# Regrouping a mixture-of-experts stage behind graph attention: two chunks and one, in place of one and two

## The chip, the cores and the metric

The kernel runs on one core of a Trainium2 chip, as one program and one launch. The metric is the device time in microseconds (us) of one execution; lower is better. Three timed runs of the kernel before gave 534.91, 538.07 and 540.5 us, so the median is 538.07 us. One more execution was recorded by the hardware profiler; every duration below comes from that one.

The engines are called as in the profile: PE (TensorE; PEld is its weight load), DVE (VectorE), ACT (ScalarE), POOL (GpSimd) and SP (SyncE, which here only issues DMAs).

## The reference, cut to what matters

A stack of four residual layers works on 1354 nodes with 128 features; `adj` is a 1354 x 1354 matrix of edge weights, none negative.

```python
x = x + gnn0(layernorm(x), adj)        # weights from adj, times a message
x = x + ffn0(layernorm(x))             # 8 experts of 256, top 2, computed densely
x = x + gnn1(layernorm(x), adj)        # two GRU cells and three heads of attention
x = x + ffn1(layernorm(x))             # 8 experts of 341, top 2

def ffn1(z):
    probs = softmax(z @ router_w.T)
    p, idx = top_k(probs, 2)
    p = p / (sum(p) + 1e-9)
    gates = one_hot(idx) weighted by p
    h = silu(z @ w1[e].T) * (z @ w3[e].T)
    return sum over e of gates[e] * (h @ w2[e].T)
```

The change concerns the last layer, `ffn1`, and how it is laid beside the attention of `gnn1`.

## The kernel before, in words

Nodes are columns. They are cut into 11 tiles of 128 (the last has 74), and the tiles into three chunks: chunk 0 is tiles 0 to 3, chunk 1 tiles 4 to 7, chunk 2 tiles 8 to 10 (330 columns). The names `mid(1, c)`, `center(3, c)` and the like carry the layer and the chunk.

**Attention.** The loop has 3 chunks x 3 heads x 11 tiles = 99 steps. A step (h, j) is one `factor` matmul on PE (L1310), one `numerator` on DVE (L2029, which multiplies by the adjacency) and one `attend` on PE (L1321, recorded as two MATMULs). `factor` runs three steps ahead; DVE writes into a ring of three. Steps (0, j) to (5, j) are chunks 0 and 1 with 512 columns, steps (6, j) to (8, j) are chunk 2 with 330. Everything else is hung onto these steps by tables written out by hand: `MAIN_PE` and `MAIN_DVE` say after which step a side task runs on its engine, and `MAIN_ACT` is ACT's plain order. Engines run in order, so a side task that waits holds up the steps behind it. Side tasks are the GRU of the node update (`gates`, `mid`, `new`, `blend`, `add`), then for each chunk the layer norm (`mean`, `center`, `var`, `scale`), the router (`logits`, `scores`, `shares`, `ranks`, `picks`, `weights`), the token-major copy (`ztok`), the counting of places (`prefix`, `slots`) and a list of blocks (`list`). `support` copies the finished sum of a chunk out of PSUM, and the first step of the next chunk waits for it.

**Experts.** Each token goes to two experts. POOL writes its row with an indirect DMA into a table in DRAM, sorted by expert: `send(t, j)` for tile t and choice j (L568). When all sends of a group of tokens have landed and its `list` is known, SP loads the table block by block, 128 rows each, at most four blocks ahead (`block_load`, L466). A block is transposed (L1377 on PE, L2047 on DVE), multiplied by w1 and w3 (L1385, L1386), goes through `silu` on ACT (L895) and a product on DVE (L2065), is transposed (L1392, L885) and multiplied by w2 (L1401). DVE scales the result by the gate (L2052, L2053) and POOL scatters it into a second table (`block_sent`, L574). In iteration b, PE does the first products of block b, then the transposes of block b + 2, then the later steps of blocks b - 1 and b - 2. The first five blocks share one pair of PSUM banks, so there the first products wait for DVE's product of the block before.

There are two groups, each with its own tables and list. Before, group 0 is chunk 0 (15 blocks) and group 1 chunks 1 and 2 (21 blocks). Chunk 1's last steps, all of chunk 2's last GRU part and both routers run beside the blocks by six further tables (`PE1A`, `PE1B` and so on, keyed by block). `SENDS` says after which block's scatter POOL makes which sends: two after each of blocks 0 to 3 and 5 to 7. At the end a group's results are read back (`fetched`, `picked_y`) and `combine` adds them to the residual (L2039, L2042); SP writes the output.

What orders the work around the change is therefore only this: the hand-written tables, each engine's own order, and semaphores. The lines of the profile that matter are L1321 and L2029 (attention), L1595 to L1664 (router, places and list), L568 and L574 (POOL), L466 (SP), L1377 to L1401 (blocks).

## Time and profile before

| what | value |
|---|---|
| median of the timed runs | 538.07 us |
| profiled execution, its own time | 539.31 us |
| span of its record | 537.6 us |
| PE busy | 449.4 us (84%) |
| DVE busy | 345.5 us (64%) |
| ACT busy | 239.4 us (45%) |
| POOL busy | 68.8 us (13%) |

The profiled execution is 1.7 us longer than its span, which is what lies around the recorded instructions, and 0.23% above the median. Busy shares are averages over all stages. The attention's last chunk runs from about 367 to 410 us, the blocks of the experts from 413 to 523 us, and the rest is the way out. PEclk in a table is the clock granted to PE, 1.00 for 2.4 GHz and 0.50 for 1.2 GHz. An idle time in square brackets stands before the instruction, with what ended it.

### The profile page before, as it was taken

Reading aid. Unit: us, or ns where it says so; the run is one execution under the profiler, and the core shown is the slowest. Engines: PE = TensorE matmul, PEld = TensorE weight load, DVE = VectorE, ACT = ScalarE, POOL = GpSimd, SP = SyncE. Lnnn points to the kernel's source line nnn. Section 1 sums busy time; section 2 is a strip of 40 time slices with the busy share of each in tenths; the row PEclk is TensorE's granted clock in tenths of the full one; section 3 lists DMA queues with packets and bytes.
Section 4 is the critical chain, followed back from the end, with each engine's and each line's share of the span. In section 5 each row is a group of like instructions: output and inputs, shape, how many; then the busy total and the mean of one; then the engine's idle time right before and its main releaser. Section 6 shows DMA issues by size and latency. Waiting matters only on the chain.

```text
span 537.6 us, 6518 instructions
## 1 busy us (share of the span) xinstructions
PE 449.4 (84%) x1858; PEld 265.5 (49%) x1858; DVE 345.5 (64%) x761; ACT 239.4 (45%) x389; POOL 68.8 (13%) x115
## 2 busy tenths in 40 slices
PE   4497679978699899989889999998799858799980
PEld 2432435535356654546434444344456546588860
DVE  0997989868478742446737877866777636355541
ACT  4988789587685522040350212212122462344430
POOL 5000000000010000000000000000140255444440
PEclk9779698989899999999999999999989979899995
DMA  8989200000000000000000004400010111123213
GB/s 283 312 262 390 84 0 0 1 0 1 1 1 1 2 0 1 0 2 1 1 0 1 0 30 160 125 20 8 11 46 15 36 54 46 43 61 99 79 37 109
DMA packets 26491, 31.22 MB, mean 58 GB/s; under 512 B 3572, under 2 KB 20781, under 8 KB 26453
## 3 DMA queue, kind: packets, MB, share of 16 engines
q1 hardware_dynamic: 23557, 26.52, 15.6%
q0 software_dynamic: 1984, 3.78, 2.1%
q10 hardware_dynamic: 912, 0.46, 0.3%
q8 instruction: 19, 0.31, 0.2%
q14 instruction: 19, 0.16, 0.1%
HBM read 19.44 MB, written 11.31 MB: 57 GB/s over the span
## 4 chain that ended last, share of the span: by engine, by line
PE 52%; DVE 24%; ACT 10%; issue 9%; another core or an unknown queue 2%; DMA 1%; POOL 1%; DVEq 0%; POOLq 0%; ACTq 0%; SPq 0%
PE bank L1321 10%; PE bank L1130 4%; PE bank L1401 4%; PE bank L1385 4%; PE bank L1269 3%; PE bank L1386 3%; DVE pr_ring L2029 3%; PE bank L1310 2%; DVE y_units L1510 2%; PE bank L1091 2%; DVE y_units L1521 2%; PE bank L980 2%; PE bank L1392 2%; DVE hr_ring L1832 2%
## 5 line engine op out<-in xcount | busy, mean ns | idle before, releaser
L1321 PE MATMUL bank<-pr_ring,hW 128*128 128x512 f32 (+3 forms) x198 | 95.0, 565 | 8.1 <-DVE pr_ring L2029 6.4
L2029 DVE SCALAR_TENSOR_TENSOR pr_ring<-adjT,regR,bank 128x512 f32<-128x512 f32 (+3 forms) x99 | 65.0, 680 | 33.2 <-PE bank L1310 31.4
L1321 PEld LDWEIGHTS bank<-pr_ring,hW 128*128 128x128 f32 (+1 forms) x198 | 35.2, 195 | 36.7 <-issue 17.5
L980 PE MATMUL bank<-y_units,msg 128*128 128x512 f32 (+3 forms) x66 | 33.2, 632 | 15.7 <-DVE y_units L1531 15.7
L1091 PE MATMUL bank<-hr_ring,W2s 128*128 128x512 f32 (+1 forms) x96 | 44.9, 555 | 0.0
L574 POOL DMA_INDIRECT yg<-pr_ring,goes x36 | 34.8, 966 | 72.9 <-DVE pr_ring L2053 71.7
L1832 DVE TENSOR_TENSOR hr_ring<-hr_ring,bank 128x512 f32<-128x512 f32 (+1 forms) x48 | 29.5, 620 | 19.3 <-ACT hr_ring L774 15.6
L2065 DVE TENSOR_TENSOR hbuf<-hbuf,bank 128x341 f32<-128x341 f32 x36 | 18.3, 509 | 33.3 <-issue 15.5
L774 ACT ACTIVATE hr_ring<-bank,b1c 128x512 f32<-128x512 f32 (+1 forms) x48 | 29.8, 628 | 14.2 <-PE bank L953 14.1
L951 PE MATMUL bank<-zhi,W1hi 128*128 128x512 f32 (+1 forms) x48 | 34.7, 723 | 1.2 <-ACT hr_ring L774 0.9
L1401 PE MATMUL bank<-wall,hturned 114*128 (+1 forms) x216 | 31.0, 280 | 1.0 <-DVE pr_ring L2053 0.9
L568 POOL DMA_INDIRECT xg<-rowx,slot x22 | 22.5, 1024 | 65.1 <-DVE slot L1642 59.0
L1385 PE MATMUL bank<-wall,xturned 128*128 x72 | 28.4, 477 | 1.4 <-DVE xturned L2047 0.6
L885 ACT COPY hturned<-bank 114x384 f32<-114x384 f32 x36 | 17.2, 479 | 26.2 <-PE bank L1392 18.2
L1401 PEld LDWEIGHTS bank<-wall,hturned 114*128 114x128 f32 (+1 forms) x216 | 27.6, 195 | 1.7 <-issue 1.7
L980 PEld LDWEIGHTS bank<-y_units,msg 128*128 128x128 f32 (+1 forms) x66 | 13.5, 218 | 28.3 <-DVE y_units L1531 19.7
L1386 PE MATMUL bank<-wall,xturned 128*128 x72 | 27.1, 458 | 0.0
L895 ACT ACTIVATE hbuf<-bank 128x341 f32<-128x341 f32 x36 | 16.4, 457 | 24.0 <-PE bank L1385 21.8
L1130 PE MATMUL bank<-adjT,hTok 128*128 128x512 f32 (+3 forms) x66 | 26.2, 545 | 0.0
L538 POOL TENSOR_SCALAR_AFFINE_SELECT adjT<-adjT 128x128 f32<-128x128 f32 (+1 forms) x11 | 3.4, 323 | 156.4 <-DVE y_units L1531 135.7
L635 ACT ACTIVATE y_units<-y_units,one 128x1024 f32<-128x1024 f32 (+3 forms) x18 | 17.6, 979 | 11.6 <-DVE y_units L1521 11.6
L1510 DVE SCALAR_TENSOR_TENSOR y_units<-adjT,y_units 128x1024 int32<-128x1024 int32 (+3 forms) x18 | 18.2, 1014 | 5.2 <-ACT y_units L630 5.2
(308 smaller groups left out, 879.3 us busy)
## 6 DMA issues: line engine op xcount, KB each, us to landing
xg<-zeros SPq DMA_DIRECT2D x1, 4095.0 KB
wall<-in_w SPq DMA_DIRECT2D x2, 1364.0 KB
adjT<-in_adjT SPq DMA_DIRECT2D x1, 2560.0 KB
xg<-zeros SPq DMA_DIRECT2D x1, 2535.0 KB
xblk<-xg SPq DMA_DIRECT2D x36, 65.0 KB
adjT<-in_adjT SPq DMA_DIRECT2D x1, 1650.0 KB
adjT<-in_adjT SPq DMA_DIRECT2D x3, 512.0 KB, 5.8
adjT<-in_adjT SPq DMA_DIRECT2D x1, 1024.0 KB
```

The costliest lines, as they stand in the source:

```text
L574: pool.indirect_dma_start(yg_d[g], bass.IndirectOffsetOnAxis(goes[:, b % YRING:b % YRING + 1], 0), yblk[:, b % YRING, :], None).then_inc(s ...
L774: nc.scalar.activation(hr_ring[:, q % RING0, 0:w], B_H[q % 3][:, 0:w], ACT.Relu, bias=b1c[:, e * M0 + m:e * M0 + m + 1]).then_inc(s["h_rel ...
L951: nc.tensor.matmul(out, whi, xhi, start=start, stop=False)
L980: mm = nc.tensor.matmul(B_GNN[:, 0:w], msg[0:r, j, :], y_units[0:r, g % RINGY, i, 0:w], start=(j == 0), stop=(j == T - 1))
L1091: nc.tensor.matmul(B_Y0[:, 0:w], W2s[:, e, m, :], hr_ring[:, q % RING0, 0:w], start=False, stop=(e == E - 1 and m == M0 - 1)).then_inc(s[" ...
L1130: ns = nc.tensor.matmul(B_NS[c][:, 0:width(c)], hTok[0:r, j, :], adjT[0:r, j, cols(c)], start=(j == 0), stop=(j == T - 1))
L1321: nc.tensor.matmul(B_ACC[:, 0:w], hW[0:r, j, k * P:(k + 1) * P], ring[0:r, 0:w], start=(k == 0 and j == 0), stop=(k == K - 1 and j == T - ...
L1385: nc.tensor.matmul(B_H1[pair(b)][:, 0:H1], x, walls[:, bass.ds(base, H1)], start=True, stop=True).then_inc(s["h1_ps"], 1)
L1386: nc.tensor.matmul(B_H3[pair(b)][:, 0:H1], x, walls[:, bass.ds(base + H1, H1)], start=True, stop=True).then_inc(s["h3_ps"], 1)
L1401: mm = nc.tensor.matmul(B_Y[:, 0:P], hturned[0:r, b % 2, k * P:(k + 1) * P], walls[0:r, bass.ds(base + 2 * H1 + k * P, P)], start=(k == 0) ...
L1832: nc.vector.tensor_tensor(hr, hr, B_GATE[q // M0 % 2][:, 0:w], ALU.mult).then_inc(s["h_gated"], 1)
L2029: nc.vector.scalar_tensor_tensor(out=pr_ring[0:r, 4 + p % R_RING, 0:w], in0=adjT[0:r, j, cols(c)], scalar=g_col[0:r, j, k:k + 1], in1=B_F[ ...
```

## The change

1. The groups become tiles 0 to 7 (chunks 0 and 1, 23 blocks) and tiles 8 to 10 (chunk 2, 13 blocks). There are still 36 blocks. The first group's results are fetched and combined at block 31 and 30 in place of 25 and 24, for eight tiles in place of four; the last `combine` takes three tiles, once, in place of four and three.
2. The router of this layer is shorter. `shares` is gone (the two largest shares are found from the logits and only their exponentials are divided by their sum), `ranks` has three instructions in place of five, the copy of the logits out of PSUM is gone, and `weights` has one more.
3. Chunk 1's last side tasks, `ztok`, `prefix`, `ranks`, `picks`, `weights`, `slots`, and the list of group 0 move from the blocks into the attention, as do chunk 1's eight sends. Chunk 0's move to earlier steps. The list is cut in two tasks, `starts` and `list`.
4. The last chunk's GRU (`last_gates`, `mid(1, 2)`) goes ahead of the first block on PE, DVE and ACT.
5. POOL makes the last chunk's six sends one at a time, after the scatters of blocks 8, 10, 12, 14, 16 and 18.

```diff
-GROUPS = [(0, 4), (4, T)]
-GROUP_OF = [0, 1, 1]
+GROUPS = [(0, 8), (8, T)]
+GROUP_OF = [0, 0, 1]
-FETCH = BLOCKS[0] + 10
+FETCH = BLOCKS[0] + 8
 MAIN_PE = {
-    (5, 10): [("ztok", 0)], (6, 4): [("gates", 1, 1)], (6, 6): [("mid", 1, 1)], (6, 8): [("prefix", 0)],
-    (7, 4): [("mean", 3, 1)], (7, 8): [("var", 3, 1)], (8, 5): [("logits", 4)],}
+    (5, 1): [("ztok", 0)], (5, 3): [("prefix", 0)], (6, 0): [("gates", 1, 1)], (6, 2): [("mid", 1, 1)], (6, 8): [("mean", 3, 1)],
+    (7, 0): [("var", 3, 1)], (7, 4): [("logits", 4)], (7, 5): [("ztok", 1)], (7, 7): [("prefix", 1)]}
 MAIN_DVE = {
...
-    (6, 9): [("mid", 1, 1)], (7, 0): [("weights", 3), ("slots", 3), ("list", 0)], (7, 2): [("blend", 1, 1)], (7, 4): [("add", 1, 1)], (7, 6): [("center", 3, 1)],
+    (6, 5): [("mid", 1, 1)], (6, 8): [("blend", 1, 1)], (6, 9): [("add", 1, 1)], (7, 1): [("center", 3, 1)], (7, 5): [("scale", 3, 1)],
+    (7, 8): [("scores", 4), ("ranks", 4), ("picks", 4)], (7, 10): [("weights", 4)], (8, 1): [("slots", 4)], (8, 3): [("starts", 0)], (8, 6): [("list", 0)]}
...
-PE1A = {0: [("mid", 1, 2)], 1: [("prefix", 1)], 4: [("var", 3, 2)], 7: [("prefix", 2)]}
-PE1B = {0: [("ztok", 1)], 3: [("mean", 3, 2)], 5: [("logits", 5), ("ztok", 2)], 9: [("xtok", 0)], 10: [("xtok", 1)], 11: [("xtok", 2)]}
+PE1A = {4: [("var", 3, 2)], 7: [("prefix", 2)]}
+PE1B = {3: [("mean", 3, 2)], 5: [("logits", 5), ("ztok", 2)], 9: [("xtok", 0)], 10: [("xtok", 1)], 11: [("xtok", 2)]}
-DVE1A = {0: [("mid_n", 1, 2)], 1: [("blend", 1, 2), ("add", 1, 2)], 3: [("slots", 4)], 6: [("ranks", 5), ("picks", 5)], 7: [("slots", 5)]}
+DVE1A = {0: [("blend", 1, 2)], 1: [("add", 1, 2)], 5: [("scores", 5), ("ranks", 5), ("picks", 5)], 7: [("slots", 5)]}
-SENDS = {b: [(4 + b, 0), (4 + b, 1)] for b in range(4)}
-SENDS.update({5 + i: [(8 + i, 0), (8 + i, 1)] for i in range(3)})
+SENDS = {8 + 2 * i: [(8 + i // 2, i % 2)] for i in range(6)}
...
-            for t in tiles(0):
+            for t in range(8):
                 for j in range(2):
                     send(t, j)
...
                 pe.wait_ge(s["tables_in"], 64 + 80)
+                last_gates()
+                mid(1, C - 1)
                 pe.wait_ge(s["list_set"], 1)
...
             def route_ranks(n):
...
+                if l:
+                    link(nc.vector.tensor_tensor(g4[0], D.unsqueeze(2).to_broadcast([P, k, E, E]), D.unsqueeze(3).to_broadcast([P, k, E, E]), ALU.subtract))
+                    link(nc.vector.tensor_tensor(g4[1], g4[0], floor1[:, :, :].unsqueeze(1).to_broadcast([P, k, E, E]), ALU.is_gt))
+                    link(nc.vector.tensor_reduce(G, g4[1], AX.X, ALU.add))
+                    return
```

On POOL, first the order before, from the end of the constants. `xg<-rowx,slot` is a send, `yg<-pr_ring,goes` the scatter of a block.

```order
L578 MEMSET place_no 128x4x8 x2
L568 DMA xg<-rowx,slot 4992x130 x8
L574 DMA yg<-pr_ring,goes 2304x128
L568 DMA xg<-rowx,slot 8064x130 x2
L574 DMA yg<-pr_ring,goes 2304x128
L568 DMA xg<-rowx,slot 8064x130 x2
L574 DMA yg<-pr_ring,goes 2304x128
L568 DMA xg<-rowx,slot 8064x130 x2
L574 DMA yg<-pr_ring,goes 2304x128
L568 DMA xg<-rowx,slot 8064x130 x2
L574 DMA yg<-pr_ring,goes 2304x128 x2
```

And the order on POOL after the change, from the same place.

```order
L574 TENSOR_SCALAR floor<-tri 128x64
L563 DMA xg<-rowx,slot 9088x130 x16
L569 DMA yg<-pr_ring,goes 2560x128 x9
L563 DMA xg<-rowx,slot 3968x130
L569 DMA yg<-pr_ring,goes 2560x128 x2
L563 DMA xg<-rowx,slot 3968x130
L569 DMA yg<-pr_ring,goes 2560x128 x2
L563 DMA xg<-rowx,slot 3968x130
L569 DMA yg<-pr_ring,goes 2560x128 x2
L563 DMA xg<-rowx,slot 3968x130
L569 DMA yg<-pr_ring,goes 2560x128 x2
L563 DMA xg<-rowx,slot 3968x130
```

Sixteen sends now stand ahead of the first scatter, and of the last group's six each has two scatters before the next; the sixth (not shown) follows the scatter of block 18.

On DVE, before the change, chunk 1's `blend` (L1922 to L1924) and `add` (L1930, L1931) in the attention, with the numerators L2029 around them.

```order
L2029 SCALAR_TENSOR_TENSOR pr_ring<-adjT,regR,bank 128x330 x2
L1922 TENSOR_TENSOR nsT<-zT,ge 128x512
L1923 SCALAR_TENSOR_TENSOR nsT<-ge,nsT 128x512
L1924 SCALAR_TENSOR_TENSOR nsT<-nsT,ge 128x512
L2029 SCALAR_TENSOR_TENSOR pr_ring<-adjT,regR,bank 128x330 x2
L1930 TENSOR_TENSOR nsT<-nsT,bank 128x512
L1931 TENSOR_TENSOR xT<-xT,nsT 128x512
```

The same piece of DVE's order after the change.

```order
L2029 SCALAR_TENSOR_TENSOR pr_ring<-adjT,regR,bank 128x330 x3
L1922 TENSOR_TENSOR nsT<-zT,ge 128x512
L1923 SCALAR_TENSOR_TENSOR nsT<-ge,nsT 128x512
L1924 SCALAR_TENSOR_TENSOR nsT<-nsT,ge 128x512
L2029 SCALAR_TENSOR_TENSOR pr_ring<-adjT,regR,bank 128x330
L1930 TENSOR_TENSOR nsT<-nsT,bank 128x512
L1931 TENSOR_TENSOR xT<-xT,nsT 128x512
```

One numerator now stands between `blend` and `add` in place of two; PE's `mean(3, 1)`, which waits for `add`, is placed after step (6, 8), one step ahead of `add`'s step, where before both stood at (7, 4).

## Rows read from the trace of the kernel before

**Rows 1.** Windows by stage: us, busy (count) of PE PEld DVE ACT POOL; PEclk, DMA, GB/s.
```profile
367.20:409.55 42.35, 36.63 (x149) 20.85 (x147) 31.60 (x82) 10.15 (x13) 8.16 (x8) 0.92 0.07 20
413.20:467.90 54.70, 41.01 (x243) 29.69 (x242) 27.88 (x105) 23.24 (x42) 23.97 (x24) 0.91 0.15 43
467.90:523.10 55.20, 54.29 (x337) 43.38 (x336) 27.56 (x96) 22.05 (x48) 24.12 (x25) 1.00 0.24 67
```

**Rows 2.** Timeline (start, us, engine, what): the list inside the attention, PE's stop.
```profile
382.82 0.22 DVE L1595 TENSOR_TENSOR chosen<-rt,place_no 128x64 f32<-128x64 f32 x1
...
388.37 0.92 PE L1321 MATMUL bank<-pr_ring,hW 128*128 128x330 f32 x1 [3.53 <-DVE pr_ring L2029]
```

**Rows 3.** Windows: the stretch behind that stop.
```profile
388.40:394.40 6.00, 6.00 (x13) 3.07 (x14) 5.62 (x10) 0.00 (x0) 4.58 (x5) 0.50 0.14 45
```

**Rows 4.** Timeline: start of chunk 2's steps, blend, add, two ordinary steps.
```profile
369.42 0.82 PE L1321 MATMUL bank<-pr_ring,hW 128*128 128x330 f32 x2 [1.59 <-ACT nsT L880]
...
388.72 0.67 DVE L1922 TENSOR_TENSOR nsT<-zT,ge 128x512 f32<-128x512 f32 x1
...
392.53 0.69 DVE L1931 TENSOR_TENSOR xT<-xT,nsT 128x512 f32<-128x512 f32 x1
...
400.98 0.30 PE L1310 MATMUL bank<-share_c,pr_ring 120*128 120x330 bf16 x1
...
401.68 0.30 PE L1310 MATMUL bank<-share_c,pr_ring 120*128 120x330 bf16 x1
```

**Rows 5.** Timeline of PE: first products of blocks 0, 4, 6, 13, 35.
```profile
413.18 0.45 PE L1385 MATMUL bank<-wall,xturned 128*128 x1
...
426.84 0.55 PE L1385 MATMUL bank<-wall,xturned 128*128 x1
...
439.72 0.93 PE L1385 MATMUL bank<-wall,xturned 128*128 x1
...
467.94 0.45 PE L1385 MATMUL bank<-wall,xturned 128*128 x1
...
517.53 0.46 PE L1385 MATMUL bank<-wall,xturned 128*128 x1
```

**Rows 6.** Chain of waits (start, us, what) in the first 14 blocks.
```profile
435.15 3.03 another core or an unknown queue
...
453.50 2.88 another core or an unknown queue
...
456.79 1.71 another core or an unknown queue
458.55 3.55 another core or an unknown queue
```

**Rows 7.** Windows: the stretch of blocks 4 to 12; the eight sends inside the attention.
```profile
426.80:462.10 35.30, 24.64 (x147) 17.46 (x147) 16.38 (x66) 14.59 (x24) 21.07 (x21) 0.90 0.17 49
386.40:396.80 10.40, 8.43 (x21) 4.33 (x22) 8.80 (x21) 0.63 (x1) 8.16 (x8) 0.67 0.14 45
```

**Rows 8.** Timeline: first and last of eight sends in a row, first block load.
```profile
386.44 1.23 POOL L568 DMA_INDIRECT xg<-rowx,slot  x1 [56.87 <-DVE slot L1642]
...
395.77 0.96 POOL L568 DMA_INDIRECT xg<-rowx,slot  x1 [0.30 <-issue]
...
399.12 0.38 SPq L466 DMA_DIRECT2D xblk<-xg  x1
```

**Rows 9.** Timeline: the scatter of block 11, two iterations later.
```profile
471.10 0.96 POOL L574 DMA_INDIRECT yg<-pr_ring,goes  x1 [1.30 <-DVE pr_ring L2053]
```

**Rows 10.** Timeline: the last scatter, the fetch, the start of combine, the last store.
```profile
523.86 0.96 POOL L574 DMA_INDIRECT yg<-pr_ring,goes  x1 [0.67 <-DVE pr_ring L2053]
...
526.39 0.38 SPq L480 DMA_DIRECT2D picked_y<-yg  x1
...
531.59 0.69 DVE L2039 TENSOR_TENSOR answer<-x3tok,picked_y 128x512 f32<-128x512 f32 x1 [8.01 <-DMA picked_y<-yg]
...
534.52 0.39 SPq L486 DMA_DIRECT2D out<-answer  x1
```

91 lines of the change are left out of this document (41 added, 50 removed).

## The prediction, made before the changed kernel was run

> **What bounds the kernel now.** I read the stage windows first, then the timeline of PE at each stage's borders, then the chain of waits inside the stage that looks worst. The windows [rows 1] show three stages. In the attention of the last chunk PE is busy 36.63 of 42.35 us, so PE sets the pace and every wait of PE costs about its length. In the first thirteen blocks PE is busy 41.01 of 54.70 us, so something else sets the pace. From block 13 on it is busy 54.29 of 55.20: pure PE, and the side tasks that remain there are hidden. The same shows in the block starts [rows 5]: 22 blocks from 467.94 to 517.53 are 2.25 us each, while the first 13 took 54.8 us, 25.5 more than 13 such blocks. The chain of waits says where much of that is [rows 6]: four times PE's work stands still for "another core or an unknown queue", 3.03 + 2.88 + 1.71 + 3.55 = 11.2 us. Nobody else works on this program. All four stand where POOL makes sends and scatters without a pause: 21 indirect DMAs in 35.3 us, 21.07 us busy [rows 7], and with the 0.30 us of issue in front of each [rows 8] that is 27.4 us, 78%. I read them as one thing: while POOL issues such a run, signals that PE sent earlier arrive late. That is an inference; the rows show only the place and the length.
>
> Inside the attention there is one plain stop [rows 2]: DVE starts weights, slots and the list of group 0 at 382.82 in one piece, and PE runs dry for 3.53 us until the numerator behind them. The six us after it run at clock 0.50 with PE busy throughout [rows 3], so half of that, 3.0 us, is lost too.
>
> **The change, part by part**, against the profiled execution's 539.31 us.
>
> *(a) The attention, chunk 2.* Out go the stop (-3.5), the slow clock behind it (-3.0), and most of the 1.59 us wait at the first step of the chunk [rows 4], since chunk 0's tasks on ACT come earlier (-1.2). In come `ztok` and an eight-tile `prefix` on PE, about ten small matmuls that overlap; from 0.30 us for one [rows 4] less the overlap I take 1.35 us, plus 0.4 for fewer steps between the waits. New waits: `mean(3, 1)` now stands on PE after step (6, 8), and `blend` starts on DVE only after that step's numerator. Between them lie three operations of blend, one numerator and two of add. A 512-wide operation is 0.67 to 0.69 us [rows 4], so about 5 x 0.67 + 0.5 = 3.9 us, while PE has three steps in hand at 0.70 us each (401.68 less 400.98 [rows 4]), the first partly spent: about 2.65 us of waiting. The DVE work moved in (route of chunk 1, slots, list) is split into pieces of about 1 to 3 us against PE's 2.1 us of steps in hand: 0.6 for `var`, 1.1 before `logits`, 1.1 for `ztok`, 1.0 for weights and slots, and 1.9 for `list`, whose one piece is the longest left. Together 8.4; each could be 0 if DVE is further ahead than I count, or 1.5 times as large, so 4 to 11. Sum of (a): -7.7 + 1.75 + 8.4 = **+2.5**. The attention ends at 412.1 and not at 409.55.
>
> *(b) End of the attention to the first product.* Before 3.63 us (413.18 [rows 5] less 409.55 [rows 1]). The slots of chunk 1 are ready at about 403.1. Eight sends took 386.44 to 395.77 for the start of the last, 9.33 us, and SP's first load came 3.35 us after that [rows 8]. So the last send starts at about 412.9, counting about half a microsecond in which POOL waits for DVE, the load is issued at 416.3, and with about 2.7 us for landing and the transpose the first product is at 419. `last_gates` and `mid(1, 2)`, about 5.6 us on PE with their waits, fill that gap up to 417.7; they cost nothing more, and would cost their length if the sends were early. Between 2 (sends in time) and 7 (POOL late), I take **+3.3**.
>
> *(c) Blocks 0 to 13.* Chunk 1's eight sends leave this stage, and so do `mid`, `ztok`, `prefix` and `slots`. POOL has in blocks 0 to 8 one scatter per block, as it has after block 13, where no such wait exists. So -11.2 for the four waits and about -1.4 for ztok and prefix on PE; another -1.9 for `mid` and the waits on it. Walking through block by block gives 40.2 us in place of 54.75: 10.9 more than steady blocks, which is what the shared pair of banks (blocks 0 to 4), three means, logits and transposes of chunk 2 need. **-14.5**. If the waits belong not to the runs of sends but to this stage, 0 to -3; if the slow clock there (PEclk 0.90 [rows 7]) goes altogether, -17.
>
> *(d) The change of group.* This is what the change newly adds. The last send follows the scatter of block 18. A scatter of block b - 2 starts 3.16 us behind the first product of block b (471.10 less 467.94 [rows 9, 5]), so with T20 the first product of block 20 the send is at T20 + 4.43, the load of block 23 at T20 + 7.8 by the 3.35 us above, and its rows are transposed and ready at about T20 + 9.75. But block 23 is the first of group 1, and PE's transposes of it are queued in iteration 21, at T20 + 2.25 + 1.15 = T20 + 3.4. PE stops for 6.4 us, with the later steps of blocks 20 and 19 queued behind; blocks 24 to 26 load meanwhile, and the fetch of group 0 isn't touched. SP's latency of 3.35 was seen behind a run of sends; behind a single one it is at least 2.3, and the landing between 0 and 3.1 us (the store at the very end takes 537.6 less 534.52 [rows 10]), of which I take 2.0: the stop is between 3.4 and 8. PE ran at 0.50 for six us after the last stop of 3.5 us [rows 3], in steps that kept it busy; a similar dip here costs 0 to 3.4, I take 2.0. **+8.4**. Before, the last group's sends ended after block 7 and its first block was 15, so no such wait shows.
>
> *(e) The end.* From the last scatter 2.53 us to the fetch, 5.2 more to the first `combine`, 2.9 to the last store and 3.1 to the end [rows 10]. Three tiles in place of seven shorten the fetch by 1.55 (the fixed part stays) and leave 1.3 us less of combine: **-3.0**, between -1.5 and -4. The earlier eight-tile fetch (double the bytes at DMA share 0.24 [rows 1]) and its combine of 1024 columns, about 2.2 us on DVE, lie beside blocks in which DVE is busy only 27.56 of 55.20 us [rows 1]: nothing, and about 2 us if one of them held PE's operands back.
>
> The shorter router saves DVE work only; beside PE-bound steps it is inside (a).
>
> Sum: 2.5 + 3.3 - 14.5 + 8.4 - 3.0 = **-3.3**, so 536.0 us. The profiled execution is 0.23% above the median of the three runs, so 534.8; I say **535.0**.
>
> **A rule weighed.** In the attention eight sends ran beside DVE busy 8.80 of 10.40 us [rows 7], each 0.96 to 1.23 us, one every 1.3 [rows 8]. By that sixteen sends inside the attention are cheap. The Trainium skill, "SBUF — State Buffer", section "SBUF: two separate sides", says the opposite can happen: descriptors of a GpSimd-issued DMA can't be written while a two-port VectorE operation holds the shared ports, and a DMA of some 620 ns then took some 3100. By that rule eight sends would take about 20 us longer and the first block with them. The trace disagrees so far, so the sum goes by the row.
>
> **The rivals.**
>
> 1. *The late signals come back between blocks 8 and 18 (slower).* There POOL makes 11 scatters and 6 sends, 17 x 1.27 = 21.6 us, in 11 blocks of 2.25 = 24.8 us: 87%, denser than the 78% at which the four waits stand [rows 7]. Against it: a run is only scatter, send, scatter. The deciding point is whether the late signals follow the share of POOL or the number of DMAs without a pause. If the share, the waits return with 8 to 11.2 us: 543 to 546. Chance 0.17, with the lags that two runs of eight sends could bring into the attention's end.
> 2. *The waits in the attention are smaller, and no slow clock follows (faster).* DVE is busy 31.60 of 42.35 us [rows 1]; if its pieces fit between the steps, (a) is -2 instead of +2.5, and (d) without the dip is +6.4: 535 - 4.5 - 2 = 528.5. Chance 0.27.
> 3. *The first blocks don't get faster.* If the four waits hang on the shared banks or on list and table, (c) gives only -3.3 and the whole is 546. Chance 0.05.
> 4. *The rule above*: some 20 us late before block 0, about 550. Chance 0.02.
> 5. *The change does nothing new at the change of group*, because SP's loads don't wait for all sends: (d) is 0, 526.6. The lists need all tokens, so 0.03.
>
> **How the numbers follow.** My forecast has the rest, 0.46, with its own range 531 to 540. What a measurement of this kernel can tell from no change is about 1%, 5.4 us: below 532.7 is faster, above 543.5 slower. Faster: 0.25 of rival 2, rival 5 wholly, and 0.09 of the forecast, 0.37. Slower: 0.09 of rival 1, and 3 and 4 wholly, 0.16. The rest, 0.47, is the same. The range from 528 to 543 leaves out most of rivals 3 to 5 and the far ends of 1 and 2.
>
> **What would show it.** (a) no DVE piece from weights to list, PE idle before `mean` at about 2.6 us and before the step behind `list` below 2; (b) first product at about 419; (c) no "unknown queue" in the chain before block 8, 13 blocks in about 40 us; (d) PE idle about 6 us before the transposes of block 23, ended by DMA or DVE's copy of it, and nothing like it elsewhere; (e) last scatter to end in about 10.7 us. Wrong would be: waits of PE between blocks 8 and 18 that no send explains, a clock of 0.50 over more than ten us, or a block 23 that finds its rows there.

## The result, and the profile after

The changed kernel took 549.31 us (median of 4, 545.81 to 550.29) where the kernel before took 537.20 us (4 runs, 534.91 to 540.50): ratio 1.0216, 95% interval 1.0173 to 1.0259. I had forecast 535.0 us, range 528 to 543: the change is slower, by 1.7 to 2.6%, and the time lies outside the range. On two other chips the ratio was 1.0211 [1.0146, 1.0277] and 1.0147 [1.0097, 1.0197], slower there too.

The windows of the changed kernel by stage: us, then busy time (count) of PE, PEld, DVE, ACT and POOL, PEclk, DMA share, GB/s. They answer to [rows 1]: the attention's last chunk, blocks 0 to 13, 13 to 21, 21 to 23, and 23 to 35.

```profile
373.60:418.25 44.65, 37.92 (x167) 21.41 (x167) 29.58 (x74) 9.64 (x12) 11.22 (x13) 0.92 0.06 18
426.10:468.20 42.10, 38.02 (x200) 27.68 (x201) 22.99 (x85) 21.02 (x38) 10.53 (x11) 0.88 0.15 39
468.20:486.30 18.10, 18.10 (x115) 14.56 (x114) 9.05 (x32) 7.50 (x17) 11.67 (x12) 1.00 0.23 65
486.30:502.10 15.80, 7.64 (x30) 5.86 (x29) 2.35 (x8) 1.87 (x4) 3.54 (x4) 0.68 0.15 38
502.10:530.70 28.60, 27.58 (x170) 21.73 (x169) 15.46 (x49) 11.23 (x24) 12.22 (x12) 1.00 0.36 100
```

The first blocks are the gain: 42.1 us where [rows 1] had 54.7. The third row is as steady as before, eight blocks in 18.1 us at clock 1.00, with the single sends beside them. The fourth row is the loss: two blocks take 15.8 us, and PE is busy for half of it at clock 0.68. The chain of waits there (start, us, what) names its links, and the timeline of PE gives the stop:

```profile
487.17 0.95 POOL yg L569
488.43 4.12 DMA xg<-rowx,slot
...
493.66 2.04 DMA xblk<-xg
495.75 0.48 PE bank L1373
```

```profile
484.58 0.74 PE L1382 MATMUL bank<-wall,xturned 128*128 x2
...
486.84 0.74 PE L1382 MATMUL bank<-wall,xturned 128*128 x2
495.75 0.48 PE L1373 MATMUL bank<-ident,xblk 128*128 128x128 f32 x1 [8.16 <-DMA xblk<-xg]
```

The last send (starts 488.43) stands behind the scatter of block 18. It lands 4.12 us after its start, SP's first load of the new group comes 5.2 us after that start, and only when its rows are there can PE transpose block 23. Before, nothing like it stood at block 15.

Ahead of the blocks, PE waits in two places. In the attention, the timeline of PE and of DVE around chunk 1's `mean`:

```profile
386.20 0.30 PE L1306 MATMUL bank<-share_c,pr_ring 120*128 120x330 bf16 x1
389.03 1.95 PE L955 MATMUL bank<-xT,meanw 128*128 128x512 f32 x2 [2.52 <-DVE xT L1931]
```

```profile
384.92 0.69 DVE L1922 TENSOR_TENSOR nsT<-zT,ge 128x512 f32<-128x512 f32 x1
...
388.28 0.69 DVE L1931 TENSOR_TENSOR xT<-xT,nsT 128x512 f32<-128x512 f32 x1
```

And windows of the two stretches in which the clock fell, as it had in [rows 3]:

```profile
388.90:393.00 4.10, 3.97 (x8) 1.98 (x9) 1.61 (x5) 0.00 (x0) 0.00 (x0) 0.58 0.00 0
402.70:406.00 3.30, 3.30 (x21) 1.99 (x19) 1.77 (x6) 2.30 (x2) 0.00 (x0) 0.52 0.02 5
```

Before the first product, POOL's eight sends and what follows them (chain of waits), and PE's own waits for the last chunk's GRU and for the first rows (timeline):

```profile
410.24 0.95 POOL xg L563
...
419.07 2.27 DMA xg<-rowx,slot
...
423.57 1.75 DMA xblk<-xg
```

```profile
422.30 0.82 PE L1185 MATMUL bank<-zT,gruw 128*128 128x330 f32 x2 [1.11 <-ACT ge L795]
...
424.36 0.30 PE L1373 MATMUL bank<-ident,xblk 128*128 128x128 f32 x1 [0.62 <-DMA xblk<-xg]
...
426.12 0.92 PE L1381 MATMUL bank<-wall,xturned 128*128 x2 [0.42 <-DVE xturned L2047]
```

The end is shorter, as forecast; the rows answer to [rows 10]:

```profile
537.01 0.96 POOL L569 DMA_INDIRECT yg<-pr_ring,goes  x1 [0.68 <-DVE pr_ring L2053]
539.46 0.38 SPq L478 DMA_DIRECT2D picked_y<-yg  x1
543.18 0.56 DVE L2039 TENSOR_TENSOR answer<-x3tok,picked_y 128x384 f32<-128x384 f32 x1 [6.44 <-DMA picked_y<-yg]
...
544.77 0.37 SPq L481 DMA_DIRECT2D out<-answer  x1
```

Stage by stage, from three traces of each kernel (the kernel before: its first trace, e9, e13; the changed one: its first, e5, e14). "Ahead" ends at the first `attend` matmul of step (2, 6), up to which both programs are the same; (a) runs from that of step (6, 0) to that of the last step.

| stage | before, us | changed, us | difference of means | forecast |
|---|---|---|---|---|
| ahead | 312.55, 313.47, 312.50 | 316.90, 313.10, 312.92 | +1.5 | 0 |
| to step (6, 0) | 56.9 each | 56.7 each | -0.2 | 0 |
| chunk 2's steps (a) | 39.41, 39.53, 38.41 | 44.07, 44.31, 44.42 | +5.2 | +2.5 |
| to the first product (b) | 4.35, 4.43, 4.43 | 8.43, 8.53, 8.55 | +4.1 | +3.3 |
| blocks 0 to 13 (c) | 54.76, 54.80, 53.36 | 42.09, 43.01, 43.09 | -11.6 | -14.5 |
| blocks 13 to 23 (d) | 22.58 each | 33.89, 33.30, 35.81 | +11.8 | +8.4 |
| blocks 23 to 35 | 27.02, 26.98, 26.98 | 28.59, 28.60, 28.65 | +1.6 | 0 |
| to the end of the span (e) | 20.03, 20.03, 19.93 | 17.12, 16.55, 16.83 | -3.2 | -3.0 |
| sum | | | +9.2 | -3.3 |

The timed runs gave 12.1, 9.7 and 8.0 us on three chips, 9.9 in the mean, so the traces hold about the whole.

### The profile page after: what moved, and what is told of

Its sections match the earlier page's. It is cut to its first block, busy times and chain, and to the rows that moved or that the text cites. A ratio compares the mean times of both kernels' runs of the same rounds, so it can differ in the third digit from the quotient of the medians.

```text
span 547.8 us, 6510 instructions
## 1 busy us (share of the span) xinstructions
PE 459.6 (84%) x1862; PEld 270.7 (49%) x1862; DVE 341.0 (62%) x744; ACT 239.7 (44%) x389; POOL 69.3 (13%) x116
## 4 chain that ended last, share of the span: by engine, by line
PE 51%; DVE 23%; ACT 10%; issue 9%; DMA 3%; POOL 3%; SPq 0%; DVEq 0%; POOLq 0%; ACTq 0%
PE bank L1317 8%; PE bank L1126 4%; PE bank L1397 4%; PE bank L1381 4%; PE bank L1382 3%; PE bank L1265 3%; DVE pr_ring L2029 3%; PE bank L976 2%; DVE y_units L1507 2%; PE bank L1087 2%; PE bank L1388 2%; PE bank L1306 2%; DVE y_units L1518 2%; DVE hr_ring L1832 2%; PE bank L1213 2%
## 5 line engine op out<-in xcount | busy, mean ns | idle before, releaser
L2029 DVE SCALAR_TENSOR_TENSOR pr_ring<-adjT,regR,bank 128x512 f32<-128x512 f32 (+3 forms) x99 | 64.7, 680 | 37.1 <-PE bank L1306 35.7
L1317 PEld LDWEIGHTS bank<-pr_ring,hW 128*128 128x128 f32 (+1 forms) x198 | 34.9, 196 | 33.6 <-DVE pr_ring L2029 15.8
L976 PE MATMUL bank<-y_units,msg 128*128 128x512 f32 (+3 forms) x66 | 34.5, 652 | 17.3 <-DVE y_units L1528 17.3
L569 POOL DMA_INDIRECT yg<-pr_ring,goes x36 | 35.3, 979 | 74.3 <-DVE pr_ring L2053 73.1
L1087 PE MATMUL bank<-hr_ring,W2s 128*128 128x512 f32 (+1 forms) x96 | 44.3, 548 | 0.0
L770 ACT ACTIVATE hr_ring<-bank,b1c 128x512 f32<-128x512 f32 (+1 forms) x48 | 29.8, 628 | 16.2 <-PE bank L949 16.1
L1381 PE MATMUL bank<-wall,xturned 128*128 x72 | 29.8, 497 | 2.3 <-DVE xturned L2047 1.3
L881 ACT COPY hturned<-bank 114x384 f32<-114x384 f32 x36 | 17.2, 479 | 32.4 <-PE bank L1388 32.4
L1382 PE MATMUL bank<-wall,xturned 128*128 x72 | 29.0, 486 | 0.0
L1126 PE MATMUL bank<-adjT,hTok 128*128 128x512 f32 (+3 forms) x66 | 27.9, 573 | 0.0
L631 ACT ACTIVATE y_units<-y_units,one 128x1024 f32<-128x1024 f32 (+3 forms) x18 | 17.6, 978 | 11.6 <-DVE y_units L1518 11.6
L1087 PEld LDWEIGHTS bank<-hr_ring,W2s 128*128 128x128 f32 x96 | 17.8, 192 | 7.6 <-issue 3.2
```

The source lines that it names most:

```text
L569: pool.indirect_dma_start(yg_d[g], bass.IndirectOffsetOnAxis(goes[:, b % YRING:b % YRING + 1], 0), yblk[:, b % YRING, :], None).then_inc(s ...
L770: nc.scalar.activation(hr_ring[:, q % RING0, 0:w], B_H[q % 3][:, 0:w], ACT.Relu, bias=b1c[:, e * M0 + m:e * M0 + m + 1]).then_inc(s["h_rel ...
L976: mm = nc.tensor.matmul(B_GNN[:, 0:w], msg[0:r, j, :], y_units[0:r, g % RINGY, i, 0:w], start=(j == 0), stop=(j == T - 1))
L1087: nc.tensor.matmul(B_Y0[:, 0:w], W2s[:, e, m, :], hr_ring[:, q % RING0, 0:w], start=False, stop=(e == E - 1 and m == M0 - 1)).then_inc(s[" ...
L1126: ns = nc.tensor.matmul(B_NS[c][:, 0:width(c)], hTok[0:r, j, :], adjT[0:r, j, cols(c)], start=(j == 0), stop=(j == T - 1))
L1317: nc.tensor.matmul(B_ACC[:, 0:w], hW[0:r, j, k * P:(k + 1) * P], ring[0:r, 0:w], start=(k == 0 and j == 0), stop=(k == K - 1 and j == T - ...
```

## The experiments

Times are medians; "before" is the kernel before on the same chip. e1 to e4 ran on one chip, e5 to e8 on a second, e9 to e12 on a third, e13 to e16 on a fourth, and e17 and e18 later on that fourth chip. e9, e11 and e12 have one time each, that of their traced execution: 540.43, 544.50 and 542.02 us, with 540.80 for the kernel before on that chip. The ratio has its 95% interval. In the code shown, entries of the hand-written tables are cut out of longer lines, and `...` marks what is left out.

| run | us | before | ratio |
|---|---|---|---|
| e1 early single sends | 539.85 | 540.14 | 1.0019 [0.9987, 1.0051] |
| e2 pairs | 540.88 | 540.14 | 1.0036 [1.0003, 1.0070] |
| e3 six at once | 542.85 | 540.14 | 1.0067 [1.0034, 1.0100] |
| e4 old groups | 542.83 | 540.14 | 1.0049 [1.0021, 1.0077] |
| e5 changed, again | 546.75 | 537.08 | 1.0211 [1.0146, 1.0277] |
| e6 spaced | 534.89 | 537.08 | 0.9983 [0.9946, 1.0021] |
| e7 GRU behind | 536.14 | 537.08 | 0.9990 [0.9951, 1.0029] |
| e8 add later | 533.78 | 537.08 | 0.9959 [0.9931, 0.9988] |
| e10 list apart | 539.04 | 540.80 | 0.9991 [0.9953, 1.0029] |
| e13 before, again | 539.32 | 540.53 | 0.9984 [0.9951, 1.0018] |
| e14 changed, again | 548.55 | 540.53 | 1.0147 [1.0097, 1.0197] |
| e15 spaced, again | 539.60 | 540.53 | 0.9974 [0.9946, 1.0003] |
| e16 slots early | 534.45 | 540.53 | 0.9908 [0.9874, 0.9942] |
| e17 both chains | 535.65 | 540.58 | 0.9909 [0.9877, 0.9940] |
| e18 slots early, again | 535.71 | 540.58 | 0.9906 [0.9874, 0.9938] |

### When the last sends come: e1, e2, e3

```diff
-SENDS = {8 + 2 * i: [(8 + i // 2, i % 2)] for i in range(6)}
+SENDS = {6 + i: [(8 + i // 2, i % 2)] for i in range(6)}          # e1
+SENDS = {8 + i: [(8 + i, 0), (8 + i, 1)] for i in range(3)}       # e2
+SENDS = {12: [(8 + i // 2, i % 2) for i in range(6)]}             # e3
```

> The changed kernel, but its last chunk's six sends follow the scatters of blocks 6, 7, 8, 9, 10 and 11 in place of 8, 10, 12, 14, 16 and 18. Theory L (the last send is too late for the next group's first load): PE's stop of 8.2 us before the transposes of block 23 and the 3 us of slow clock behind it vanish, block 23's first product comes 22.6 us after block 13's in place of 33.9, and the time is 11.3 us below the changed kernel's, about 538. Rival R (a run of back-to-back indirect DMAs on POOL makes PE's signals late; here twelve follow each other from block 6 on): the gain is eaten by waits of 5 to 11 us between blocks 8 and 13, and the time stays at 543 to 549. Rival G (the change of group costs by itself, by its list and first load): the stop stays above 4 us, about 545.

> The changed kernel with the last chunk's sends in pairs after the scatters of blocks 8, 9 and 10, as the kernel before pairs its own. Theory L: the last send still ends some 20 us before block 23 is needed, so the same gain of 11.3 us as with early single sends, about 538. Rival R: nine indirect DMAs in a run delay PE's signals, and blocks 9 to 13 take 3 to 9 us more than the 11.1 us they took; then single sends are worth something by themselves, and this run is slower than the one with early single sends by that much.

> The changed kernel with all six sends of the last chunk in one run after the scatter of block 12, with the late scatters behind them. The last send is then at about 8 us after the first product of block 14 and so some 8 us ahead of need: theory L gives the same 11 us of gain, about 538. Rival R: this is the longest run in this stage, six sends and four late scatters; PE's signals come 2 to 6 us late from the fifth on and PE stops for 3 to 9 us near blocks 15 to 17: 541 to 547. If a run alone doesn't do it, blocks 13 to 23 stay at 2.26 us each.

In all three the stop before block 23 is gone, and with it the slow clock behind it: theory L holds, rival G falls. But blocks 13 to 23 take 25.7, 27.8 and 29.4 us where PE alone needs 22.6, and in e1 blocks 8 to 13 take 1.2 us more than in the other two. The excess grows with the length of the run of sends: 4.3, 5.2 and 6.8 us. The medians go the same way, though the intervals of neighbours overlap. The three also differ in where the run stands.

POOL and PE of e3 (timelines) show how it looks. Six sends and two scatters follow each other at 0.30 us, and PE stops twice with "issue" as the only releaser:

```profile
474.60 0.96 POOL L563 DMA_INDIRECT xg<-rowx,slot  x1 [0.30 <-issue]
...
481.30 1.34 POOL L563 DMA_INDIRECT xg<-rowx,slot  x1 [0.30 <-issue]
482.95 0.98 POOL L569 DMA_INDIRECT yg<-pr_ring,goes  x1 [0.30 <-issue]
```

```profile
479.64 0.51 PE L1388 MATMUL bank<-ident,hbuf 128*114 128x128 f32 x3 [1.26 <-issue]
482.52 1.47 PE L1397 MATMUL bank<-wall,hturned 114*128 x6 [2.37 <-issue]
```

The semaphore events that PE's own instructions send at their end stand in the trace 2.6 to 6.3 us behind that end there; these are the late signals. The transposes at L1388, for one, end at 476.44, their event stands at 478.99, and the copy on ACT that waits for it (L881) starts at 479.01. DVE's and ACT's own events in this stretch are not late where the trace has them. The latest event of PE is 2.0 us late in e1, 4.6 in e2 and 6.3 in e3; in the changed kernel's first trace, in e5 and in e6 none is 0.5 us late.

So rival R is right in kind beside theory L. Its sizes were not, but for e3 (542.85, said 541 to 547): e1 was to be 538 by L alone, and 543 to 549 by R, with waits of 5 to 11 us between blocks 8 and 13; it is 539.85, with 1.2 us there and 3.1 behind. In e2, at 540.88, nothing was lost in blocks 9 to 13, where R had put 3 to 9 us. How far each lies below the changed kernel goes by the ratios alone, as that kernel did not run on this chip.

### The old groups: e4

```diff
-GROUPS = [(0, 8), (8, T)]
-GROUP_OF = [0, 0, 1]
+GROUPS = [(0, 4), (4, T)]
+GROUP_OF = [0, 1, 1]
-SENDS = {8 + 2 * i: [(8 + i // 2, i % 2)] for i in range(6)}
+SENDS = {5 + i: [(8 + i, 0), (8 + i, 1)] for i in range(3)}
```

> The changed kernel with the groups of the kernel before (tiles 0 to 3, and 4 to 10), all else as changed but the last chunk's sends, in pairs after blocks 5, 6 and 7 as before: the regrouping alone is undone. Theory C (the first product of block 0 waits for the chain from chunk 1's slots through eight sends, 16.2 us, and not for PE): the first product comes 3 to 4 us earlier, right behind the last chunk's GRU; the stop at the change of group is gone or below 2 us; the last combine takes seven tiles and gives 3 us back; about 549.3 - 3.5 - 11 + 3 = 538. If PE and the last gates bound the first product, it doesn't move (less than 1 us), about 541. Rival R: eight sends beside the first blocks bring late signals, 5 us and more.

The stop is gone (blocks 13 to 23: 22.6 us), blocks 23 to 35 are back at 27.0 and the end at 20.9. But theory C fell: the first product comes 8.47 us behind the attention's last step, as in the changed kernel (8.43), although it needs no send of chunk 1. Its trace goes there through the gates on ACT and `mid`. Blocks 0 to 13 took 47.5 us and not 43: late signals (events of PE up to 6.5 us behind), with the six sends in pairs after blocks 5 to 7, somewhat less than the 5 us and more of rival R. The time was to be 538 to 541 and is 542.83.

### The changed kernel again, and the spaced sends: e5, e6

> The changed kernel once more, unaltered. Its first trace lies 4.35 us behind that of the kernel before already at step (2, 6) of the attention, where both programs are the same. Theory N (that is chance: the clock falls to 0.50 at other moments in each execution): the offset at that step is another one here, between 0 and 5 us. Theory S (it belongs to the changed kernel): it is 4 us again. The stop before block 23 comes again in the same place, 8 us, and the stretch from block 13 to block 35 takes 62 us again. Time 1.7 to 2.6% above the kernel before.

e5: ahead of step (2, 6) it is only 0.5 us behind the first trace of the kernel before, and from there to the end 231.0 us, as in its first trace (230.9). So the 4.35 us of the first trace don't come each time (theory N). That all of it is chance doesn't follow: see "Ahead" below.

```diff
-SENDS = {8 + 2 * i: [(8 + i // 2, i % 2)] for i in range(6)}
+SENDS = dict(zip((6, 8, 9, 11, 12, 14), [[(t, j)] for t in (10, 8, 9) for j in range(2)]))
-DVE1B.setdefault(FETCH - AHEAD + 3, []).append(("combine", 0, 0))
+for i in range(2):
+    DVE1B.setdefault(FETCH - AHEAD + 3 + i, []).append(("combine", 0, i))
...
```

> The changed kernel with two edits: the six sends follow the scatters of blocks 6, 8, 9, 11, 12 and 14, one each, tile 10's (74 rows) first, so that at most three or four indirect DMAs follow each other without a pause; and the first group's combine of 1024 columns is cut in two of 512, one block apart. Theory L + R (a late last send costs 11.3 us; a long run of indirect DMAs costs late signals): no stop at the change of group, block 6 to 35 takes 67 to 69 us with late signals under 2 us in all, where early single sends took 76.6; the step from block 32 to 33 is 2.3 us in place of 3.8. In all 5 to 7 us less than with early single sends, 533 to 535, that is 0.8 to 1.2% below the kernel before. Rival (late signals come with any sends in these blocks): 3 to 5 us of them stay, about 538.

e6 is 11.9 us below e5 on the same chip, and its trace from step (2, 6) on 11.7 us below. Against its own forecast it fell short: blocks 6 to 35 took 71.2 us, not 67 to 69, and it lies 0.2% below the kernel before, within the noise, not 0.8 to 1.2%. The windows of blocks 13 to 23 show where the 11.7 us are. First e6, then e5:

```profile
465.40:487.90 22.50, 22.50 (x142) 18.08 (x141) 11.32 (x40) 9.28 (x21) 13.26 (x14) 1.00 0.25 72
```

```profile
465.70:498.90 33.20, 24.91 (x142) 19.60 (x141) 11.40 (x40) 9.26 (x20) 15.20 (x15) 0.85 0.19 53
```

The same 142 instructions of PE take 22.5 us without a gap in e6, and 33.2 in e5, of which PE is idle 8.3 and 2.4 us slower by the clock. The combine in two pieces brought blocks 23 to 35 from 28.6 to 27.5 us, 0.5 above the kernel before; I had said 2.3 us for one block, and it moved to the next, 33 to 34 (2.7 us).

### Two chains before the first product: e7, e16, e17, e18

```diff
-                mid(1, C - 1)                                      # e7, e17
-PRE_ACT = [("support", 2), ("gates", 1, 2), ("new", 1, 2)]
+PRE_ACT = [("support", 2), ("gates", 1, 2)]
-PRE_DVE = [("mid", 1, 2)]
+PRE_DVE = [("mid_r", 1, 2)]
+PE1A = {0: [("mid", 1, 2)], ...
+ACT1A = {0: [("new", 1, 2)]}
-DVE1A = {0: [("blend", 1, 2)], 1: [("add", 1, 2)], ...
+DVE1A = {0: [("mid_n", 1, 2)], 1: [("blend", 1, 2), ("add", 1, 2)], ...
```

```diff
-(7, 7): [("prefix", 1)]                                            # e16 to e18, on e8
+(7, 6): [("prefix", 1)]
-(7, 10): [("weights", 4)], (8, 1): [("slots", 4)], (8, 3): [("starts", 0)], (8, 6): [("list", 0)]
+(7, 9): [("weights", 4)], (7, 10): [("slots", 4)], (8, 2): [("starts", 0)], (8, 5): [("list", 0)]
```

> As the spaced kernel, and the last chunk's mid(1, 2) goes back behind the first products of block 0, as in the kernel before. With the old groups the first product came at the same distance behind the attention as in the changed kernel, though it needed no send of chunk 1: its chain went through the gates on ACT and mid. Theory T (two equally long chains lie before the first product, the eight sends and the GRU): this edit alone moves the first product by less than 0.7 us, and as mid's 1.5 us of PE now lie behind block 0 the whole is 0 to 1.5 us slower than the spaced kernel. Rival (only the GRU sets the start): 2 to 3 us faster.

> As the kernel with add one numerator later (e8), and chunk 1's prefix on PE after step (7, 6), its weights on DVE after (7, 9), slots after (7, 10), starts after (8, 2), list after (8, 5): each one step earlier. Theory T (sends and GRU are two equally long chains before the first product): slots come about 1 us earlier and the first product less than 0.7 us earlier. Rival (the sends alone set it): a full 1 us and more earlier. Either way within 0.3% of e8.

> As e16 (slots early), and the last chunk's mid(1, 2) behind the first products of block 0 as in e7. Theory T (two equally long chains lead to the first product, and e16 shortened one, e7 the other): only now the first product comes earlier by 1.5 to 3 us, 104.6 to 106.1 us after step (2, 6) in place of 107.6; blocks 0 to 13 take up to 1.5 us longer as mid lies there; in sum 0 to 2 us less than e16. Rival (a third chain, the loads of the blocks or PE's own gates, is as long): under 0.7 us earlier, and the sum 0.5 to 1 us more.

> The kernel e16 again, unaltered, as the counterpart of e17 on the same chip, and as the best version so far for a second measurement: 0.8 to 1.2% below the kernel before if e16's figure holds, within 0.5% if it was the chip's.

From step (2, 6) to the first product e6 took 109.5 us and e7 109.6: moving the GRU alone gives nothing, as theory T said, and in all e7 is 1.2 us slower than e6. In e16 the first of chunk 1's sends starts 2.7 us earlier than in e8 (89.6 and 92.4 us after step (2, 6)), but the first product only 0.6 us (107.6 and 108.2); the same program in e18 had it at 106.3. By e16 that is theory T, by e18 its rival. In e17 it came at 106.1, where theory T wanted 104.6 to 106.1: between 0.2 and 1.5 us of gain from the second chain, and none in the time (535.65 us beside e18's 535.71). PE waited there 0.5 us for rows and 1.2 us for DVE's copy of them. e4, which needs no send of chunk 1, and e7, which has the GRU later, each leave the first product where it was, so two chains of about equal length stood before it; what bounds it once both are shorter is not shown.

### The stop before mean: e8

```diff
-(6, 8): [("mean", 3, 1)], (7, 0): [("var", 3, 1)]                 # PE
+(6, 10): [("mean", 3, 1)], (7, 1): [("var", 3, 1)]
-(6, 9): [("add", 1, 1)]                                            # DVE
+(6, 10): [("add", 1, 1)]
```

> As the spaced kernel, and in the attention chunk 1's add is one numerator later on DVE (after step (6, 10)), its mean on PE after step (6, 10) and var after (7, 1). Theory W (PE's idle 2.5 us before mean costs also the slow clock of about 4 us behind it, 2 us of loss): the stop falls below 1.3 us, PE keeps its clock, the attention ends 1.5 to 3.5 us earlier, and the first product 0 to 2 us earlier, as the sends' chain starts from slots. Rival (the chain of chunk 1 is bound by DVE and ACT, not by where PE stops): the stop reappears before logits or ztok, no gain above 0.7 us.

The stop of 2.5 us is gone, and other waits grew: 1.6 us before logits (1.3 in e6) and 2.1 for numerators (1.4). The attention's steps took 43.4 us and not 44.3: 0.9 us, between theory W (1.5 to 3.5) and its rival (under 0.7). The larger part of its gain stands elsewhere: blocks 0 to 13 took 39.5 us where e6 took 43.1. The windows of that stage, e8 and then e6:

```profile
423.60:463.10 39.50, 35.08 (x200) 26.27 (x201) 22.97 (x85) 21.00 (x38) 12.52 (x13) 0.96 0.16 43
```

```profile
422.30:465.40 43.10, 39.20 (x201) 28.82 (x202) 22.96 (x85) 21.03 (x38) 12.54 (x13) 0.84 0.15 39
```

The same work, with PEclk 0.96 in place of 0.84. In e8 the clock had been at 0.50 for about ten us before (398 to 408), within the attention, so theory W's "PE keeps its clock" is wrong too. The timed gain of e8 over e6 is 0.24% only, with overlapping intervals. And e16 and e18, one and the same program, took 39.7 and 43.3 us for these blocks at PEclk 0.96 and 0.85. So a difference of 3.6 us here needs no edit.

### The kernel before: e9, e10, e13

> The kernel before once more, unaltered, for one profile. Its late signals stood in four waits (11.2 us) between blocks 4 and 13. Theory R (they belong to the long runs of POOL's indirect DMAs): they come again, 8 to 12 us, blocks 0 to 13 take 52 to 56 us. Rival (they were chance in one execution): under 4 us, and the stretch takes 43 to 47 us; then my term for the first blocks rested on one trace only. The place of step (2, 6) was 312.55 us; by the chance of the clock it is now between 311 and 317.

e9: the late signals come again, in the chain of waits of its trace:

```profile
436.25 3.03 another core or an unknown queue
...
454.65 3.58 another core or an unknown queue
...
458.64 1.72 another core or an unknown queue
...
460.40 2.83 another core or an unknown queue
```

11.2 us once more, in the four places of [rows 6]; blocks 0 to 13 took 54.8 us. They belong to the program; in e13 they are 11.1 us. Only PE's events are late in these traces, by up to 6.0 us.

```diff
-(7, 0): [("weights", 3), ("slots", 3), ("list", 0)]
+(7, 0): [("weights", 3)], (7, 1): [("slots", 3)], (7, 9): [("list", 0)]
```

> The kernel before with one edit in DVE's table: weights stay after step (7, 0), slots come after (7, 1), and the list of group 0 after (7, 9). My prediction held that the one piece of DVE work costs 3.5 us of stop and 3.0 us of slow clock behind it. Theory P (both go): the stop falls below 1.5 us, no stretch at 0.50 between steps (7, 1) and (8, 0), the attention's last chunk takes 34 to 36 us in place of 39.4, the whole 4 to 5 us less (0.8 to 1% faster). Rival Q (the clock falls anyway, behind another of the small waits, as it did twice in the changed kernel; only the stop is saved): 37 us, the whole 1.5 to 3 us less.

The windows of e10 (the attention's last chunk, and a stretch of the first blocks):

```profile
369.40:406.60 37.20, 33.50 (x141) 18.74 (x142) 30.67 (x80) 8.60 (x11) 7.96 (x8) 1.00 0.08 22
...
416.00:424.00 8.00, 7.13 (x45) 5.59 (x46) 5.50 (x18) 3.21 (x7) 0.96 (x1) 0.79 0.04 11
```

Neither theory holds as it stood. The attention kept its clock (1.00), as P said, and still took 37.2 us, as Q said: the one stop of 3.5 us became 2.1 of waits for numerators and 0.9 of "issue". PE's busy time fell from 35.3 to 33.5 us, so the slow clock had cost 1.8 us there, not 3. In [rows 3] DVE is busy 5.62 of the 6.00 us, so at the full clock it might have set the pace; that is read from one row and was not tried. And a fall of the clock came 30 us later instead, beside blocks 1 to 3, which gave 1.3 us back. The timing shows no difference (0.9991), where both theories wanted 1.5 to 5 us.

> The kernel before, unaltered, beside the changed one on the same chip. Theory A (the stages differ by 5.8 us, the rest is the clock in unchanged stages): from step (2, 6) to the end its trace takes 225 us again, late signals in the same four places, and its step (2, 6) comes at 312.5 to 313.5 us. Rival B (on some chips the late signals or the slow stretches of the kernel before are smaller): from step (2, 6) to the end 219 to 222 us.

> The changed kernel, unaltered, beside the kernel before on the same chip. Theory A: from step (2, 6) to the end 231 us again (230.9 and 231.0 so far), step (2, 6) at 313 to 317 us, 2 us and more behind the kernel before in the mean. Rival B: that step lies within 1 us of the kernel before's, and the stages behind it hold the whole difference of 10 to 12 us.

> The spaced kernel, unaltered. If the late signals between blocks 13 and 18 are chance or come with the chip, they are here 0 or about 3 us; if the spacing keeps them away, 0 again, and the stretch from block 13 to 23 takes 22.6 us. Time 1.8 to 2.3% below the changed kernel in either case.

e13 and e14, both kernels on one chip: up to step (2, 6) they lie 0.4 us apart, and behind it 222.5 and 234.1 us, 11.6 apart. So rival B is nearer: the stages hold the difference, and the kernel before varies from one trace to the next by its clock (38.4 and 53.4 us in (a) and (c), against 39.5 and 54.8). In e14 the single sends after every second block cost 1.9 us between blocks 13 and 21, where the first trace and e5 show nothing. e15: the spaced sends, without late signals in e6, e7 and e8, cost 3.8 us here, and 3.1 to 3.8 in e11, e12, e16, e17 and e18. Spacing alone doesn't keep them away on every chip. e15 is 1.6% below e14, less than the 1.8 to 2.3% expected.

### Extra sends in a quiet stretch: e11, e12

On the spaced kernel, with a last wait for the extra sends to land:

```diff
+                for t, j in {25: [(5, 0), (5, 1), (6, 0), (6, 1)]}.get(b, []):               # e11
+                for t, j in {24: [(5, 0)], 26: [(5, 1)], 28: [(6, 0)], 30: [(6, 1)]}.get(b, []):   # e12
+                    send(t, j)
```

> The spaced kernel with four extra sends in one run after the scatter of block 25, where POOL otherwise makes one scatter per 2.26 us and PE is busy without a gap. They write rows again that hold the same data and that nobody reads any more. Theory R (a run of five and more indirect DMAs without a pause makes PE's signals late): PE's updates come 2 to 5 us late behind the fourth or fifth, and PE loses 2 to 6 us between blocks 27 and 31. Rival (it takes something of the first blocks, as the side tasks or the loads of the list): nothing, 2.26 us a block.

> The spaced kernel with the same four extra sends, one after each of the scatters of blocks 24, 26, 28 and 30. Theory R: POOL is as much busy in sum, but no more than two or three indirect DMAs follow each other; no late signal above 1 us that PE waits for, and 2.26 us a block. Rival (the share of POOL's time counts): the same loss as with the run of four, spread out.

Blocks 23 to 35 took 32.1 us with the run of four and 29.0 with four singles, where e6 took 27.5: 4.5 and 1.5 us for the same four DMAs, with PE's events up to 5.0 and 1.4 us late. One trace each, and the two times differ the same way, by 2.5 us. Theory R is right in the direction (a send in a run costs PE three times as much as one alone), wrong in that singles cost nothing. PE's stop in e11:

```profile
510.87 0.52 PE L1392 MATMUL bank<-ident,hbuf 128*114 128x128 f32 x3
513.77 1.63 PE L1401 MATMUL bank<-wall,hturned 114*128 x6 [2.38 <-issue]
```

## Why the prediction was wrong

**The mechanism that decides was in it, as (d), and was mis-sized, and nearly every other term erred to the same side.** Taking (d) away (e6, which also cuts the combine and spaces the sends) returns 11.9 us of timed difference on one chip and 9.0 on another (e15 below e14), and the kernel is then level with the one before (0.9983 and 0.9974). In the traces about 1 us of it is the combine. I had (d) at 8.4; it is 11.8 in the mean.

- **(d), +3.4. The step that failed is "the load of block 23 at T20 + 7.8 by the 3.35 us above".** T20 + 4.43 for the last send was right to 0.01 us (488.43 less 484.01). The stop was 8.16 us, not 6.4, and above my bound of 8: from the last send's start to the first load I took 3.35 us from [rows 8], a whole tile's, and it was 5.23, as this send landed after 4.12 us where a whole tile's took 2.27 (419.07). It is tile 10's, with 74 rows, and the runs tell that this goes with the tile and not with the place. In the five traces that have all landings, tile 10's two sends land 3.6 to 3.8 and 4.1 to 4.2 us after their start, also in e6, e7 and e8, where they stand first of the six; the sends of whole tiles take 2.3 to 2.9. In all twenty traces tile 10's sends hold POOL for 1.34 to 1.36 us, which the trace before showed already, beside 0.96 for a whole tile:

```profile
459.87 1.34 POOL L568 DMA_INDIRECT xg<-rowx,slot  x1 [0.30 <-issue]
```

  The change leaves these slowest sends last, where a group now waits for them, and 1.85 us of the stop hang on that. The load landed in 2.04 us as assumed. The slow clock behind the stop cost 3.2, and I had taken 2.0 out of 0 to 3.4. The mean over three traces is higher still by the late signals of e14.
- **(a), +2.7. What failed is "the slow clock behind it (-3.0)".** PEclk was 0.91 over 39.4 us before and is 0.92 over 44.1: the clock fell again, behind the new waits, for 6.8 us in two stretches where it had been 6.9 in one. So PE's busy time grew by 2.1 us (35.3 to 37.4), where I had it fall by 1.25. The waits came out better than I said: PE's idle time in these steps grew by 2.6 us (4.1 to 6.7), where I had 4.9 (8.4 in, 3.5 out); the wait before `mean` was 2.52 for 2.65. And the 1.2 us that I took off for the wait at the chunk's first step were 0.2 in the time up to there, though that wait fell from 1.59 to 0.53. e10 shows that even where the clock doesn't fall, not 3 us but about 2 come back in these steps, and that a fall is not taken out with the stop it stands behind: there it came 30 us later.
- **(c), +2.9.** The late signals went as forecast (11.2 us, confirmed by e9). What failed is the walk through the blocks at full clock (40.2 us): it fell in the changed kernel, which took 42.1 at PEclk 0.88 and 43.0 and 43.1 in its other traces. Traces in which it nearly held, of variants with nearly the same work, took 39.5 and 39.7 (e8 and e16, 0.96).
- **(b), +0.8.** The chain from slots was right in length (16.2 us for 15.9), but slots were ready 8.3 us before the attention's end and not 9.0. "They cost nothing more" of the GRU was right by luck of two equal chains (e4, e7).
- **Blocks 23 to 35, +1.6.** I had put the combine of 1024 columns at nothing, and at 2 us if it held PE's operands back. It did: the iteration that holds the combine takes 3.77 us in place of 2.26, and on DVE its two operations stand in a row before the product and the copy that PE needs next:

```profile
520.70 1.21 DVE L2039 TENSOR_TENSOR answer<-x3tok,picked_y 128x1024 f32<-128x1024 f32 x1
...
521.95 1.23 DVE L2042 TENSOR_TENSOR answer<-answer,picked_y 128x1024 f32<-128x1024 f32 x1
```

- **(e)** was right: -3.2 for -3.0. **Ahead**, three traces differ by +1.5 in the mean; all sixteen traces of the changed kernel and its variants lie between 312.8 and 316.9, the three of the kernel before and e10's between 312.5 and 313.5. The three lowest of the twenty are all of the kernel before or e10, which chance alone gives seldom; so a part may belong to the program. How, is open.

Rival 1 (late signals between blocks 8 and 18) was nearly absent in the changed kernel itself: 0, 0 and 1.9 us. It has come in its variants with denser sends. Rival 2 was half right: the waits in the attention were smaller, and the slow clock followed all the same. One sign of being wrong came as well: the clock stood at 0.50 for ten us, from 491.6 to 501.8, from inside the stop to block 23. Rival 4, the rule of the Trainium skill, "SBUF — State Buffer", on GpSimd-issued DMAs beside two-port VectorE operations, did not show: sends beside DVE busy 3.8 of 4.0 us took 0.95 to 0.96 us each. That is no test of it, as no row shows that any of these operations is of the two-port kind; my "the trace disagrees" said too much.

How I judged it: each term had its bounds; the upper ones of (a), (b), (d) and (e) together give +7.5 us and 545.6, above my range. I added middles, and all terms that the clock enters lean the same way, because I gave back the old slow stretches and priced new ones at a part. The range treated them as independent.

**A version that beats both**: e16 (spaced sends, combine in two, add later, slots earlier), 0.9908, and 0.9906 when measured again on the same chip, 2.6% below the changed kernel there (534.45 and 548.55 us). It lies 0.9% below the kernel before, beyond the noise, and on one chip only. It was to be within 0.3% of e8, whose ratio on another chip was 0.9959.

## What to carry to other kernels

When work is regrouped, write down for every new boundary when the last producer ends and when its first consumer stands in the in-order queue; here one line of a table, which looked like spreading out sends, cost 11 us in the traces. Where the last transfers gate a whole group, look at which of them is slow, and don't put it last. Do not credit the end of a slow clock to a stop that is removed, unless the stretch was bound by the engine whose clock it is and no other wait remains. Here indirect DMAs from POOL were cheapest for PE far apart: what a run of them costs stands in no queue's busy time, but in PE stops whose releaser the profile doesn't name.
